# Eight transformer sub-blocks on one core: linear attention's block takes in the expert rows' return and the normalisation

## What is computed

```python
x = x + _L0_ffn_ref(_layernorm(x, axis=-1), ...)     # one of 8 experts per row, times its probability
x = x + _L1_xattn_ref(_layernorm(x, axis=-1), ctx_1024, ...)
# _L1_xattn_ref, 16 heads of 64, 128 random features:
q = jnp.einsum('bld,dhk->blhk', query_input, Wq)
k = jnp.einsum('bld,dhk->blhk', source_input, Wk)
v = jnp.einsum('bld,dhk->blhk', source_input, Wv)
qp = _relu_kernel(q, proj)                            # relu(ratio * x . proj) + EPS
kp = _relu_kernel(k, proj)
kvs = jnp.einsum('blhm,blhd->bhmd', kp, v)
num = jnp.einsum('blhm,bhmd->blhd', qp, kvs)
den = jnp.einsum('blhm,bhm->blh', qp, jnp.sum(kp, axis=1))
att = num / den[..., None]
return jnp.einsum('blhd,hdk->blk', att, Wo)
```

## Time and profile before

| | us |
|---|---|
| median of 3 runs (2508.03 to 2517.11) | 2511.17 |
| the profiled execution's own time | 2512.5 |
| its span, first to last instruction | 2510.8 |
| TensorE busy / VectorE / ScalarE / GpSimd | 2160.3 / 1554.1 / 1403.2 / 959.8 |
| experts' last addition ends | 490.9 |
| normalisation block begins | 492.9 |
| first key product of linear attention | 511.5 |
| last output of linear attention added | 1116.9 |

### The profile page before, as it was taken

One profiled execution on the slowest core, in us unless ns is written; L12 is line 12 of the kernel. 1 busy time (PEld: TensorE's weight loads), 2 busy tenths in 40 slices (PEclk: granted clock), 3 DMA queues, 4 the chain that ended last, 5 costly groups with the idle time before them and its releaser, 6 DMA issues. The chain is left out here.

```text
span 2510.8 us, 62752 instructions
## 1 busy us (share of the span) xinstructions
PE 2160.3 (86%) x24002; PEld 1468.2 (58%) x24002; DVE 1554.1 (62%) x3659; ACT 1403.2 (56%) x3008; POOL 959.8 (38%) x1064
## 2 busy tenths in 40 slices
PE   4899579689999999978899999999974974999755
PEld 2566346367777777756656666666652642666533
DVE  3567583475655666548877777777756544655463
ACT  3566663365555555536576666666663543666542
POOL 3453133154544544424423333333333733433043
PEclk8899789899999999988999999999986995999867
DMA  5565271310000000011100000000023234333133
GB/s 124 105 119 92 86 243 41 97 52 15 8 14 15 14 8 8 2 35 64 35 8 14 9 15 15 9 16 8 2 87 106 75 87 105 86 76 70 45 100 112
DMA packets 118582, 139.60 MB, mean 56 GB/s; under 512 B 15072, under 2 KB 107184, under 8 KB 118288
## 3 DMA queue, kind: packets, MB, share of 16 engines
q1 hardware_dynamic: 110900, 115.39, 18.0%
q0 software_dynamic: 7392, 20.19, 2.6%
HBM read 93.25 MB, written 17.47 MB: 44 GB/s over the span
## 5 line engine op out<-in xcount | busy, mean ns | idle before, releaser
L1114 DVE TENSOR_REDUCE a_mx<-a_pair 112x2 f32<-112x750 f32 x256 | 237.8, 936 | 174.9 <-PE a_pair L1183 174.9
L1422 POOL TENSOR_TENSOR a_kp<-a_kp 125x512 f16<-125x512 f32 x192 | 217.7, 1158 | 259.2 <-ACT a_kp L1513 259.2
L475 POOL TENSOR_SCALAR a_space<-a_space,a_inv 112x375 f32<-112x375 f32 x256 | 148.4, 593 | 384.0 <-DVE a_inv L620 384.0
L1052 ACT ACTIVATE a_PT<-a_pair 125x672 f32<-125x672 f32 x256 | 186.2, 730 | 83.0 <-PE a_pair L1195 81.2
L513 ACT ACTIVATE a_space<-a_space,a_least 112x375 f32<-112x375 f32 x256 | 153.4, 600 | 141.1 <-DVE a_least L615 141.1
L615 DVE CUSTOM_DVE_ANT_0 a_space<-a_s,a_mask_add 112x375 f32<-112x375 f32 x256 | 130.2, 547 | 81.7 <-PE a_s L759 79.3
L1556 DVE SCALAR_TENSOR_TENSOR a_k<-a_p,a_k 128x375 f16<-128x375 f32 x128 | 69.3, 547 | 139.0 <-ACT a_k L1469 139.0
L1513 ACT CAST a_kp<-a_kp 125x512 f16<-125x512 f32 x192 | 110.3, 617 | 76.9 <-DVE a_kp L1575 76.9
L734 PE MATMUL a_p<-w_wv,w_kc 128*125 128x512 f16 x576 | 144.6, 387 | 6.1 <-DVE w_v L654 5.0
L720 PE MATMUL a_p<-w_kc,w_wk 128*128 128x375 f16 x768 | 144.3, 323 | 4.2 <-PEq L43 2.3
L1655 PE MATMUL a_p<-a_kc,a_wk 128*128 128x375 f16 x768 | 142.2, 326 | 6.3 <-POOL a_kc L1414 6.3
(11 more groups left out here) (459 smaller groups left out, 5343.0 us busy)
## 6 DMA issues: line engine op xcount, KB each, us to landing
a_kc<-in_ctxT SPq DMA_DIRECT2D x48, 375.0 KB, 6.2
a_k<-a_k_parts SPq DMA_DIRECT2D x192, 93.8 KB
w_stage<-in_L_ffn_W SPq DMA_DIRECT2D x32, 512.0 KB
w_stage<-in_L_ffn_ew SPq DMA_DIRECT2D x16, 512.0 KB
w_stage<-expert_rows SPq DMA_DIRECT2D x16, 448.0 KB, 7.9
a_v_in_sb<-in_ctx SPq DMA_DIRECT2D x16, 375.0 KB
w_kc<-in_ctxT SPq DMA_DIRECT2D x16, 375.0 KB, 3.1
a_q<-a_q_parts SPq DMA_DIRECT2D x48, 112.0 KB, 3.7
```

The lines of the kernel that those rows point to most:

```text
L475: pool.tensor_scalar(P[:, p % 4, r, :], P[:, p % 4, r, :], inv[:, p % 4, r:r + 1], 1.0, ALU.mult, ALU.mult).then_inc(P_done, 1)
L1052: act.activation(PT[:, p % 4, :, :], pair_bank[slot["turned", p]][0:KP, :, 0:KT * S], ACT.Exp).then_inc(exp_done, 1)
L1114: dve.tensor_reduce(mx[:, b % 2, 2 * pair:2 * pair + 2], pair_bank[slot["score", p]][0:S, :, 0:SK], AX.X, ALU.max).then_inc(max_done, 1)
L1422: pool.tensor_tensor(kp16[:, LO, j, hf, r, :, :].rearrange("p c m -> p (c m)"), kp[:, n % 4, :], kp16[:, HI, j, hf, r, :, :].rearrange("p ...
```

## The change

The return of the expert rows, the normalisation and the first keys are put into one block. `experts_phase` gets `finish`, false for this sub-block: it ends once the scatters are written and the weights are split. The weights of the rows move to a tile that outlives it. `Returning` fetches and adds the rows in linear attention's block, group by group; `Normalised` does the normalisation there, in slots 0 to 9. The first pair's queries move to slots 8 to 15 and their features to slots 11, 13, 15 and 18. The value weights are split ahead of the query weights, and both inside the slots. The selector pieces are made in slots 8 to 23, the second context is split in slots 10 and 11 instead of 2 and 4. The normalised rows share their space with the output weights, which are therefore fetched after the last turn; turned rows go through the three banks of sums, ratios and denominators.

```diff
+    def turn_part(self, pe, g, c, rows_done, count, taken):
+        pe.wait_ge(rows_done, count)
+        if taken:
+            pe.wait_ge(self.act_taken, taken)
+        for t in range(GT):
+            mm = pe.transpose(self.banks[g][c][:, t * S:(t + 1) * S], self.xn[:, g * GT + t, c * 128:(c + 1) * 128],
+                              self.ident[0:S, 0:S])
+        mm.then_inc(self.turned, 1)
...
+class Returning:
...
+    def load(self, sp, g):
+        rows = B * S
+        for k in range(self.K):
+            sp.dma_start(self.got[:, k, g * GT:(g + 1) * GT, :],
+                         self.ytd[k * (rows + 1):k * (rows + 1) + rows, :].rearrange("(b s) d -> s b d", s=S)[
+                             :, g * GT:(g + 1) * GT, :]).then_inc(self.got_in[g], 16)
+    def add(self, dve, g):
+        dve.wait_ge(self.got_in[g], 16 * self.K)
+        for k in range(self.K):
+            for i, b in enumerate(range(g * GT, (g + 1) * GT)):
+                if k > 0:
+                    dve.wait_ge(self.added, self.K * GT * g + (k - 1) * GT + i + 1)
+                dve.scalar_tensor_tensor(out=self.X[:, b, :], in0=self.got[:, k, b, :], scalar=self.weights[k][:, b:b + 1],
+                                         in1=self.X[:, b, :], op0=ALU.mult, op1=ALU.add).then_inc(self.added, 1)
+        dve.wait_ge(self.added, self.K * GT * (g + 1))
...
+    QF_FIRST = (11, 13, 15, 18)
...
-            if b % QB == 0:
+            if b == 0:
+                found += [("q", 0, t - 8)] if 8 <= t < 16 else []
+                found += [("qf", 0, QF_FIRST.index(t))] if t in QF_FIRST else []
+            elif b % QB == 0:
...
-        layernorm_phase(nc, tag + "n", X, XT, ident, fetch=fetch, prepare_act=prepare_act)
...
             def _(sp):
+                returning.load(sp, 0)
+                sp.dma_start(staged[:, 0, :, :], chunked(Wk)).then_inc(wk_in, 16)
+                load_context(sp, 0)
+                for r in range(2):
+                    sp.dma_start(pp[64 * r:64 * r + 64, :], projT).then_inc(pp_in, 16)
+                for g in range(1, G):
+                    returning.load(sp, g)
+                sp.dma_start(staged[:, 2, :, :], chunked(Wv)).then_inc(wv_in, 16)
+                sp.dma_start(staged[:, 1, :, :], chunked(Wq)).then_inc(wq_in, 16)
+                load_context(sp, 1)
+                sp.wait_ge(norm.turned, 2 * G)
+                sp.dma_start(wo, chunked(Wo)).then_inc(wo_in, 16)
...
-                for h in range(H):
-                    row = 32 * (h % 4) + 8 * (h // 4)
-                    pool.tensor_copy(sel[:, h // 2, h % 2 * DH:(h % 2 + 1) * DH],
-                                     ident[:, row:row + 1].to_broadcast([128, DH])).then_inc(sel_made, 1)
                 for s in steps:
+                    if 8 <= s < 8 + H:
+                        h = s - 8
...
-                    if s % SLOTS == 4 and s // SLOTS + 1 < B:
+                    if s % SLOTS == (4 if s >= SLOTS else 11) and s // SLOTS + 1 < B:
                         split_context(s // SLOTS + 1)
...
+                norm.begin_act(act)
+                act.wait_ge(wk_in, 16)
+                act.mul(wk16[:, HI, :, :], staged[:, 0, :, :], WS).then_inc(wk_hi, 1)
                 high_context(0)
-                act.wait_ge(rest_in, 48)
+                act.wait_ge(pp_in, 32)
                 act.mul(pp16[:, HI, :], pp[:, :], RATIO * WS).then_inc(pp_hi, 1)
-                act.wait_ge(w_in, 32)
-                act.mul(wq16[:, HI, :, :], staged[:, 1, :, :], WS).then_inc(w_hi, 1)
-                high_x(0)
-                act.mul(wv16[:, HI, :, :], staged[:, 2, :, :], WS).then_inc(w_hi, 1)
                 for s in steps:
+                    if s == 0:
+                        norm.root(act, 0)
+                        norm.root(act, 1)
+                        norm.normalise_act(act, 0)
+                    if s == 2:
+                        norm.root(act, 2)
+                        norm.normalise_act(act, 1)
+                    if s == 3:
+                        act.wait_ge(wv_in, 16)
+                        act.mul(wv16[:, HI, :, :], staged[:, 2, :, :], WS).then_inc(w_hi, 1)
+                    if s == 4:
+                        norm.root(act, 3)
+                        norm.normalise_act(act, 2)
+                        norm.take_act(act, 0, 0, 0)
+                        norm.take_act(act, 0, 1, 1)
+                        high_x(0)
+                    if s == 6:
+                        norm.take_act(act, 1, 0, 2)
+                        norm.take_act(act, 1, 1, 3)
+                        act.wait_ge(wq_in, 16)
+                        act.mul(wq16[:, HI, :, :], staged[:, 1, :, :], WS).then_inc(w_hi, 1)
+                    if s == 8:
+                        norm.take_act(act, 2, 0, 4)
+                    if s == 9:
+                        norm.take_act(act, 3, 0, 6)
...
+                norm.begin(dve)
+                returning.add(dve, 0)
+                norm.statistics(dve, 0)
+                norm.aggregate(dve, 0)
                 dve.wait_ge(wk_hi, 1)
...
                 for s in steps:
+                    if s in (0, 2, 4):
+                        g = s // 2 + 1
+                        returning.add(dve, g)
+                        norm.statistics(dve, g)
+                        norm.invert(dve, g - 1)
+                        norm.aggregate(dve, g)
+                        norm.shifts(dve, g - 1)
+                    if s == 5:
+                        dve.wait_ge(w_hi, 1)
+                        dve.scalar_tensor_tensor(wv16[:, LO, :, :], staged[:, 2, :, :], WS, wv16[:, HI, :, :], ALU.mult,
+                                                 ALU.subtract).then_inc(w_split, 1)
+                    if s == 6:
+                        norm.invert(dve, 3)
+                        norm.normalise_dve(dve, 3)
+                    if s == 7:
+                        low_x(0)
+                        dve.wait_ge(w_hi, 2)
+                        dve.scalar_tensor_tensor(wq16[:, LO, :, :], staged[:, 1, :, :], WS, wq16[:, HI, :, :], ALU.mult,
+                                                 ALU.subtract).then_inc(w_split, 1)
+                    if s == 8:
+                        norm.take_dve(dve, 2, 1, 5)
+                    if s == 9:
+                        norm.take_dve(dve, 3, 1, 7)
...
-                pe.wait_ge(rest_in, 48)
                 for s in steps:
+                    if s == 4:
+                        norm.turn_part(pe, 0, 0, norm.act_rows, GT, 0)
+                        norm.turn_part(pe, 0, 1, norm.act_rows, GT, 0)
+                    if s == 6:
+                        norm.turn_part(pe, 1, 0, norm.act_rows, 2 * GT, 0)
+                        norm.turn_part(pe, 1, 1, norm.act_rows, 2 * GT, 1)
+                    if s == 7:
+                        norm.turn_part(pe, 2, 0, norm.act_rows, 3 * GT, 2)
+                        norm.turn_part(pe, 2, 1, norm.act_rows, 3 * GT, 3)
+                    if s == 8:
+                        norm.turn_part(pe, 3, 0, norm.dve_rows, GT, 4)
+                    if s == 9:
+                        norm.turn_part(pe, 3, 1, norm.dve_rows, GT, 5)
...
-                for g in range(G):
+                for g in range(G if finish else 0):
```

## The result

| | before | after |
|---|---|---|
| median of 20 runs of each, us | 2509.14 (2504.70 to 2517.64) | 2519.59 (2512.12 to 2526.07) |
| ratio of the times, 95% interval | 1 | 1.0038 [1.0028, 1.0047] |
| profiled execution, its own time | 2512.5 | 2525.6 |
| its span | 2510.8 | 2523.9 |

A forecast was written before the change was run, and what follows sets the result against it. TensorE was taken to set the pace behind slot 18, so only its first sums counted: 551.9 + 1.0 − 545.1 = +7.8 us, from the median 2511.2 to 2519.0. Likeliest case 2514 to 2524; 8 in 10 range 2508 to 2526.

The forecast's parts named there:

- The whole change is worth what it does to that one time: Linear attention: only the start of TensorE's first sums (slot 18), 545.13 us before, counts; the part behind stays alone.
- The start of the block: From the experts' last scatter to the first key: block begins at 481.1, first key at 494.2, 17.3 us earlier.
- the boundary: Between the experts' block and linear attention's: costs 2.0 us as today, from 479.1 to 481.1.
- The ladder: Slots 0 to 4: VectorE and ScalarE wait on each other in order; VectorE idles 11.4 us, done at 518.55.
- Slots 5 to 7: One queue of VectorE work, 10.75 us including 0.5 for standing behind GpSimd once, to 529.3.
- Slots 8 to 15: VectorE has 17.7 us of work and 6.4 of waits; first sums come at 551.9.
- The clock term: Slots 8 to 15: one value product at the lower clock level, partly hidden, adds 1.0 us.
- VectorE never waits: Rival, slots 0 to 15: VectorE's 17.8 us of idle time vanishes; about −9 us, 2502; chance 0.10.
- faster than before once less than about 10 is left: Between 494 and 553: of VectorE's 17.8 us idle time, under about 10 must remain to beat the kernel before.
- The pauses do not come: Rival, slots 8 to 15: the 6.4 us of waits and 1.0 for the clock vanish; +0.4, 2511.6; chance 0.20.
- The clock stays low: Rival, slots 8 to 15: six values take 2.82 instead of 1.4 us; about +15, 2526; chance 0.12.
- GpSimd in the way: Rival: query input, query weights and two output weight pieces each wait behind a low feature piece; +3, 2522; chance 0.05.

The follow-up runs named there:

- late_key: Changed kernel with TensorE waiting for the second group's means before its first key product: 2508.24 us against 2496.83 for the kernel before.
- keys_first: Changed kernel with ScalarE taking two keys ahead of the next root and four rows in slots 0, 2, 4: 2494.62 us against 2496.83 before, ratio 0.9995.
- no_add: Changed kernel without 12 of the 16 additions of returned expert rows: 2504.34 us against 2496.83 for the kernel before, ratio 1.0023.
- norm_early: Changed kernel with the last group's inversion and four rows moved on VectorE from slot 6 to slot 5: 2523.68 us against 2513.41 before.
- values_first: Changed kernel with ScalarE taking values ahead of the previous slot's high features in slots 8 to 15: 2515.71 us against 2513.41 before.
- wo_later: Changed kernel with the two output weight splittings moved from slots 12 to 15 to slots 20 to 23: 2498.80 us against 2497.54 before.
- after_again: The changed kernel run and profiled again without any edit: 2505.97 us against 2496.83 for the kernel before, ratio 1.0034.
- norm3_act: Changed kernel with the last group's four rows normalised by ScalarE in slot 7 instead of VectorE in slot 6: 2504.50 us against 2497.54 before.
- boundary: Changed kernel whose experts' block also fetches the first quarter of rows, unused, and waits for it before ending: 2516.66 us against 2497.54 before.
- best: Changed kernel with keys and values earlier on ScalarE, output weights, last rows and turned groups later: ratios to before 0.9960 and, on another chip, 0.9987.

## Why the prediction was right, point by point

In the changed profile's own times less the 1.3 us by which its experts end later:

| step | forecast | measured |
|---|---|---|
| block begins | 481.1 | 482.8 |
| first key | 494.2 | 495.2 |
| VectorE idle before keys 0, 2, 3, 4 | 2.7, 2.7, 1.9, 4.15 | 2.65, 2.65, 1.61, 4.11 |
| key 4 taken from | 518.1 | 518.75 |
| VectorE ready for slot 8 | 529.3 | 531.15 |
| from there to first sums | 22.6, and clock 1.0 | 22.06 |
| first sums | 551.9, and clock 1.0 | 553.2 |

- **Where the time is decided.** "The whole change is worth what it does to that one time": held. From first sums on all fourteen executions lie within 2.6 us, with no order that follows the kernels, and late_key showed the other half of it: the first key's own time is worth little (1.4 of 3.7).
- **The start of the block.** The term mis-sized is the boundary: 3.7 us and not 2.0, 1.7 more, the largest single error. The first rows landed 4.19 after their issue (4.6 forecast), the key weights 6.15 after theirs at 484.49 (6.8 forecast: 481.6 to 488.4), which gave 0.7 back: first key 1.0 late.
- **The ladder.** Right in mechanism and to 0.3 us in each wait, and shown to be the cause by keys_first (its removal brings slot 8 forward by 9.3 to 9.4) and no_add (VectorE's queue is the path).
- **Slots 5 to 7.** The second step off: "0.5 for standing behind GpSimd once". The four normalised rows, 1.38 alone (norm_early), took 3.12 beside GpSimd's 2.31: 1.74 and not 0.5. I had looked for this only at instructions with two inputs in SBUF; these rows have one. The Trainium skill, SBUF — State Buffer, section "Who interferes with whom", holds the case that I passed over: it lists `tensor_scalar` among the operations that can take the pair of ports shared with GpSimd, when their operands meet the conditions of a mode that uses two ports. 1.38 against 3.12 agrees with it; whether these rows ran in such a mode no run here shows. But norm_early shows that the sum would not have gained by the right size taken alone: without the meeting, a key wait and the next meeting fill the time.
- **Slots 8 to 15.** Waits of 0.65, 0, 1.53, 0.72, 1.81 and 0.91 at the six values, 5.6 in all; forecast 0.8, 0, 1.7, 0.6, 2.3 and 1.0, 6.4. Their cause, ScalarE's order, is shown by values_first (5.6 to 1.7). What the walk had differently from the rows is the end: it went along VectorE's queue through both output weight pieces and the wait for value (2,1), and took 1.5 off. By the rows of wo_later's section TensorE waits for VectorE last at 548.23 and needs 6.3 from there, beside these pieces. The size is right (22.06 and 22.6), the last 6 us of the path are TensorE's own.
- **The clock term** was not needed in the first execution. In slots 8 to 15 the granted clock is 1.00, and the value products take 1.46 to 1.51 each, in the full level. 1.0 us was put there, 0 was found. It stood in the sum for the 1.2 that slots 5 to 7 took more. In after_again it came, and in its size: granted clock 0.50 and 0.55 up to 532, one value product of 2.14, 0.92 more in slots 8 to 15. In keys_first, no_add, late_key, norm3_act and boundary (22.02 to 22.06) it did not.
- **The sum.** Errors of +1.7 (boundary), −0.7 (landing), −0.35 (ladder), +1.2 (slots 5 to 7), −0.5 (slots 8 to 15) and −1.0 (clock): +0.3, against 551.9 and 1.0. The size came out near because they nearly cancel, not because each was right. The distance says +8.1 and +8.9 in the two executions, the timed ratios +9.5 and +8.5 us.

Rivals: *VectorE never waits* fell by the waits, 16.6 us; keys_first is what it would be with 8.4 us less of them. It gives 67.95, 1.3 under before, and a time that is not told from before's: with about 8 left it agrees with the point named in advance ("faster than before once less than about 10 is left"), and does not prove it. *The pauses do not come*: they came. *The clock stays low*: not in the slots where it counts, but for the one value of after_again. It is low in the ladder (granted 0.60 from 496 to 504 us and 0.50 from 512 to 520; the first 24 key products take 6.89, and 12 more at 503.98 take 2.10), where VectorE is not waiting for TensorE. *GpSimd in the way*: in one place, for 1.74, and not in four.

What stays open: what the 2 us are that the boundary waits for behind the last scatter; why the clock fell in after_again and not in after, behind the same wait of 2.73 us; and why best's first comparison gave −10 us where its distance gives −5.

## What to carry to other kernels

Work moved out of a prologue into slots of in-order queues must be priced by the order in each queue it enters: here 16 us of an earlier start were worth nothing, and whether six short reads on ScalarE stood ahead of or behind its three groups of four normalised rows was worth 9 us. Walk the two queues that hand on to each other step by step; the ladder's waits came out to 0.3 us each, those of slots 8 to 15 to 0.5. Look for the last point at which the end of the path still waits for another engine: work taken off behind it (both pieces of VectorE in wo_later) is worth nothing. And do not count a relief in the middle of such a chain at its full length: four reliefs of 1.7 to 3.9 us brought between nothing and 2.5.

## What the runs showed of the hardware that I had not expected

- The boundary between blocks is no constant: 0.8, 2.0, and 3.7 us right behind a scatter by GpSimd, of which about 1.8 ran beside another transfer (boundary).
- Beside GpSimd's feature subtractions, four VectorE rows with one input in SBUF took 3.12 us for 1.38, and a subtraction of 128x448 with two took 1.35 to 1.42 for 0.61. Removing one such meeting made the next.
- A transfer of 448 KB in rows of 1 KB landed 4.19 us after its issue (3.95 to 4.57 in the thirteen executions of kernels with it), and the 1 MB of key weights queued behind it 6.15 after theirs (6.04 to 6.75), only 0.35 more than the 5.8 without it.
- The same wait of TensorE, 2.73 us for the same rows, was followed by a granted clock of 0.50 to 0.55 (525 to 532 us) in after_again and by 1.00 in after.
